# A selective-scan layer: partial sums of its products made by an accumulating DMA, in a new order

## The chip, the cores and the metric

One Trainium2 chip, of which the kernel uses one core. The time is the device time of one execution in microseconds (us), as the median of several runs. TensorE, VectorE (DVE), ScalarE (ACT), GpSimd (POOL) and SyncE (SP) each run their own list of instructions in order and wait for each other on semaphores.

## The reference, cut to what matters

2048 tokens (2 sequences of 1024) with 128 features pass through four layers, each followed by a layer norm. The first is a Mamba layer, and most of the time goes there:

```
x_and_res = x @ in_proj_w.T;  xi, res = split(x_and_res)          # 256 channels each
xi = silu(causal_depthwise_conv(xi));  dt, Bm, Cm = split(xi @ x_proj_w.T)
delta = softplus(dt @ dt_proj_w.T + dt_proj_b)
for each token t:  h = exp(delta_t * A) * h + delta_t * Bm_t * xi_t     # 256 channels x 16 states
                   y_t = sum over the 16 states of h * Cm_t
y = (y + xi * D) * silu(res);  return y @ out_proj_w.T
```

Then come a small quantised matmul, a second state layer with one shared set of 16 states, and a network of experts: a router (softmax, the two largest of 8), for each expert gelu(h Wg) * (h Wu) Wd, and a side network for tokens beyond an expert's capacity.

## The kernel before, in words

The tokens are cut into 4 chunks of 512, with the channels or features on the 128 partitions. A chunk's Mamba layer has 2 halves of 128 channels with 16 states each: 32 units, `g = 32 * chunk + k`, 128 in all. One unit is:

- GpSimd `step` (L999): drive = du * B row, a 128x512 product, into one of 6 buffers (`DRIVES`)
- ScalarE `step` (L865): decay = exp(delta * rate), into one of 3 PSUM banks `ps_state` (`RING`)
- VectorE `step` (L1127): the scan over the 512 tokens, into `ps_state`, or into `drive` where GpSimd multiplies
- VectorE `finish` (L1144), or GpSimd `multiply` (L1020) for every fourth unit of chunk 0 and every third of the others (`MULTIPLIED`): product = state * C row, into `product[:, g % 8]`. In chunks 0 and 2 the last state is also copied into `carry` (L1140, L1023)
- TensorE `finish` (L626): adds the product to the sum over the states by a matmul with the identity, in the PSUM bank `ps_y`. An addition is two matmul records in the trace. After 16 of them VectorE's `gated` (L1150) takes the sum

A product buffer is free for unit g + 8 when TensorE has added unit g (`added`). B and C rows are copied to all partitions by DMAs of SyncE (L524), two units to a transfer, 128 x 2 x 512 x 4 bytes = 512 KB, with 4 buffers each; SyncE waits for a free C buffer before it issues the next B row.

Around this run `pre` (what the scans need), `tail` (16 steps: out projection, norms, second and third layer, router), `gate`, `up` and `down` with VectorE's `join` (L1298) and `accum` (L1311) (the experts and the side network, 9 networks a chunk), and `fin` (last norm and store). Names such as tail 2.11 mean step 11 of chunk 2; gate 2.0 is the first gate of chunk 2, and it needs tail 2.13's logits, which need the normalised tokens of tail 2.11, transposed (tail 2.11 of TensorE, L683) and copied (tail 2.12 of ScalarE, L789). A decay of ScalarE needs the bank that the product three units before has read.

What order the parts take on each engine is written out in a table, `PLACES`: for each part of each chunk a list of places, and `run` sorts all parts of an engine by them. They are ranks and no times. With `PAIRED` empty, `pair` does nothing in this kernel, and `absorbed` and `paired` are false for all units.

Of the kernel before, what the change touches and what calls it, by code (L numbers as in the profile page):

```python
# [11 lines left out]
ALU = mybir.AluOpType  # L12
# [8 lines left out]
CHUNKS = TOKENS // CHUNK  # L21
# [21 lines left out]
PAIRED = (NONE, NONE, NONE, NONE)  # L43
# [18 lines left out]
for _k, _w in PARAMS.items():  # L62
# [130 lines left out]
    },  # L193
}
# [1197 lines left out]
```

## Time and profile before

| | |
|---|---|
| median of 3 runs | 480.37 us (479.71 to 483.02) |
| the profiled execution's own time | 480.05 us |
| its span, first to last instruction | 478.3 us |
| mean granted clock of TensorE, as a share of 2.4 GHz | 0.934 |
| busy: TensorE, VectorE, ScalarE, GpSimd | 407.7, 408.9, 319.4, 230.5 us |
| units of the first layer | 128, from about 35 to 378 us of the span |

The profile is of one execution. All durations in it stand against its own time of 480.05 us, of which 1.75 us lie outside the span. Busy time of an engine says how much it does, not whether anybody waits for it; that is read from the waits and from the stages.

### The profile page before, as it was taken

The page shows a single profiled execution, that of the slowest core. Times are in us where ns is not written, and L with a number is a line of the kernel's source. Part 1 is how long each engine was busy: PE and PEld are TensorE (multiplying, and loading weights), DVE is VectorE, ACT ScalarE, POOL GpSimd, SP SyncE. Part 2 cuts the span into 40 slices and gives each one's busy share as a digit, 9 for nine tenths or more (in the row PEclk, how much of TensorE's full clock was granted, in tenths as well). Part 3 has the DMA queues.
Part 4 walks back from the last instruction along what each step waited for, and adds up shares of the span by engine and source line. Part 5 has one row for each costly group of instructions (what it writes and reads, how often), then busy time and mean ns, then how long its engine had stood idle before and what let it go on. Part 6 is the DMA issues. An engine that isn't in the chain of part 4 may idle for free.

```text
span 478.3 us, 6017 instructions
## 1 busy us (share of the span) xinstructions
PE 407.7 (85%) x1680; PEld 246.4 (52%) x1680; DVE 408.9 (85%) x890; ACT 319.4 (67%) x521; POOL 230.5 (48%) x203
## 2 busy tenths in 40 slices
PE   4989777679268999999967799999496999999993
PEld 3333222243124777755423478766132687778873
DVE  4569999999999999999999889999989765675654
ACT  3887246458544999999963778874746579587231
POOL 0049599899574475456964724656962000000000
PEclk9989989999597999999997599999789899999997
DMA  8496398998245455556853723575750000000000
GB/s 288 168 332 223 110 302 292 320 311 277 86 176 187 166 175 177 181 161 194 275 185 105 248 88 120 165 229 158 251 200 2 0 1 0 3 0 23 1 1 22
DMA packets 22065, 74.19 MB, mean 155 GB/s; under 512 B 2320, under 2 KB 4368, under 8 KB 21648
## 3 DMA queue, kind: packets, MB, share of 16 engines
q1 hardware_dynamic: 22032, 73.82, 46.7%
q8 instruction: 13, 0.21, 0.2%
q14 instruction: 20, 0.16, 0.1%
HBM read 72.50 MB, written 1.31 MB: 154 GB/s over the span
## 4 chain that ended last, share of the span: by engine, by line
PE 50%; DVE 26%; issue 11%; ACT 7%; POOL 4%; DMA 2%; SPq 1%; DVEq 0%; ACTq 0%; POOLq 0%
PE ps_g L719 11%; PE ps_y L626 10%; PE ps_u L764 10%; DVE ps_state L1127 7%; PE ps_u L719 6%; DVE product L1144 4%; PE ps_state L719 2%; DMA hidden<-w_up 2%; DVE drive L1127 2%; POOL drive L999 2%; DVE delta L1111 2%; DVE delta L1113 2%; PE ps_y L764 1%; POOL product L1020 1%; DVE stats L1154 1%
## 5 line engine op out<-in xcount | busy, mean ns | idle before, releaser
L999 POOL TENSOR_TENSOR drive<-du,b_row 128x512 f32<-128x512 f32 x128 | 164.9, 1308 | 51.0 <-DVE ps_state L1127 37.3
L626 PE MATMUL ps_y<-product,par 128*128 128x512 f32 x256 | 135.6, 648 | 21.1 <-DVE product L1144 12.7
L865 ACT ACTIVATE ps_state<-delta,decay_rate 128x512 f32<-128x512 f32 x128 | 85.5, 688 | 58.3 <-DVE product L1144 45.2
L626 PEld LDWEIGHTS ps_y<-product,par 128*128 128x128 f32 x256 | 47.9, 204 | 81.8 <-issue 32.7
L782 ACT ACT_TABLE_LOAD x69 | 88.5, 1283 | 1.9 <-PEq L1385 0.7
L1020 POOL TENSOR_TENSOR product<-drive,c_row 128x512 f32<-128x512 f32 x38 | 48.4, 1274 | 55.3 <-DVE drive L1127 51.3
L1144 DVE TENSOR_TENSOR product<-ps_state,c_row 128x512 f32<-128x512 f32 x90 | 60.2, 679 | 1.3 <-PE ps_y L626 1.0
L764 PEld LDWEIGHTS ps_u<-wd,hidden 128*128 128x128 f32 x448 | 53.8, 192 | 4.9 <-issue 2.0
L1127 DVE TENSOR_TENSOR_SCAN ps_state<-ps_state,carry,drive 128x512 f32<-128x512 f32 x44 | 55.3, 1274 | 0.3 <-ACT ps_state L865 0.3
L1127 DVE TENSOR_TENSOR_SCAN ps_state<-ps_state,drive 128x512 f32<-128x512 f32 x46 | 54.6, 1213 | 0.9 <-ACT ps_state L865 0.8
L764 PE MATMUL ps_u<-wd,hidden 128*128 128x128 f32 x448 | 54.9, 276 | 0.0
L1311 DVE SCALAR_TENSOR_TENSOR acc<-ps_u,net_weight,acc 128x128 f32<-128x128 f32 x128 | 35.7, 342 | 8.3 <-PE ps_u L764 8.0
L958 ACT ACTIVATE gelu<-ps_g 128x512 f32<-128x512 f32 (+1 forms) x42 | 24.6, 595 | 21.4 <-PE ps_g L719 17.1
L719 PE MATMUL ps_g<-hn_part,wg 128*128 128x512 f32 x114 | 34.4, 419 | 0.0
L1298 DVE TENSOR_TENSOR hidden<-gelu,ps_g 128x512 f32<-128x512 f32 x36 | 24.4, 683 | 11.7 <-PE ps_g L719 4.8
L719 PE MATMUL ps_g<-hn_part,wu 128*128 128x512 f32 x108 | 33.2, 419 | 0.1
L983 POOL TENSOR_TENSOR du<-delta,u 128x512 f32<-128x512 f32 x8 | 10.6, 1330 | 33.8 <-DVE delta L1116 33.3
L1127 DVE TENSOR_TENSOR_SCAN drive<-ps_state,carry,drive 128x512 f32<-128x512 f32 x20 | 25.4, 1271 | 0.0
L719 PEld LDWEIGHTS ps_g<-hn_part,wg 128*128 128x128 f32 x114 | 21.0, 190 | 7.6 <-ACT gelu L958 1.3
L719 PEld LDWEIGHTS ps_g<-hn_part,wu 128*128 128x128 f32 x108 | 19.3, 190 | 6.3 <-issue 1.8
L1127 DVE TENSOR_TENSOR_SCAN drive<-ps_state,drive 128x512 f32<-128x512 f32 x18 | 21.8, 1210 | 0.0
L1298 DVE TENSOR_TENSOR hidden<-gelu,ps_u 128x512 f32<-128x512 f32 (+1 forms) x24 | 16.3, 679 | 6.0 <-PE ps_u L719 3.8
(253 smaller groups left out, 600.5 us busy)
## 6 DMA issues: line engine op xcount, KB each, us to landing
b_row<-bc_dram SPq DMA_DIRECT2D x64, 512.0 KB, 5.0
c_row<-bc_dram SPq DMA_DIRECT2D x64, 512.0 KB, 4.1
x_in<-x_t SPq DMA_DIRECT2D x4, 256.0 KB, 6.9
gelu<-w_gate SPq DMA_DIRECT2D x1, 1024.0 KB, 9.1
hidden<-w_up SPq DMA_DIRECT2D x1, 1024.0 KB, 10.9
wd<-w_down SPq DMA_DIRECT2D x1, 1024.0 KB, 12.8
out<-acc SPq DMA_DIRECT2D x4, 256.0 KB, 2.4
par<-params SPq DMA_DIRECT2D x1, 598.0 KB, 6.6
```

Of the source, the lines that this page charges most:

```text
L626: mm(ps_y[:, :], ident, product[:, g % PRODUCTS, :], start=False, stop=(n == STATE - 1)).then_inc(y_pe, 1)
L719: last = mm(net_bank(c, e, kind, f)[:, :], w_in[kind][wp][:, e, f * P:(f + 1) * P], hn_parts[hp][:, :], start=(i == 0), stop=(i == 2))
L764: last = mm(block_of(out_bank(c, e)[:, :], j), hidden[:, m % 2, f, j * P:(j + 1) * P], wd[:, e, f, :], start=(f == 0), stop=(f == 1))
L782: nc.scalar.preload_act_table_set(name)
L865: nc.scalar.activation(ps_state[g % RING][:, :], delta[:, c % 2, h, :], ACT.Exp, scale=decay_rate[:, h, n:n + 1]).then_inc(decay_act, 1)
L958: nc.scalar.activation(gelu[0:rows, m % GROUP, f, :], net_bank(c, e, "wg", f)[0:rows, :], ACT.Gelu).then_inc(gelu_act, inc)
L999: nc.gpsimd.tensor_tensor(drive[:, g % DRIVES, :], du[:, h, :], b_row[:, m % ROWS, n % 2, :], ALU.mult).then_inc(drive_pool, 1)
L1020: nc.gpsimd.tensor_tensor(product[:, g % PRODUCTS, :], drive[:, g % DRIVES, :], c_row[:, m % ROWS, n % 2, :], ALU.mult).then_inc(product_p ...
L1127: v.tensor_tensor_scan(drive[:, g % DRIVES, :] if multiplied(g) else state[:, :], state[:, :], drive[:, g % DRIVES, :], 0.0 if first else ...
L1144: v.tensor_tensor(product[:, g % PRODUCTS, :], state[:, :], c_row[:, m % ROWS, n % 2, :], ALU.mult).then_inc(product_dve, 1)
L1298: v.tensor_tensor(hidden[0:rows, m % 2, f, :], gelu[0:rows, m % GROUP, f, :], net_bank(c, e, "wu", f)[0:rows, :], ALU.mult).then_inc(hidde ...
L1311: last = v.scalar_tensor_tensor(acc[:, j, :], block_of(out_bank(c, e)[:, :], j), net_weight[:, j, e:e + 1], acc[:, j, :], ALU.mult, ALU.add)
```

## The change

`SUMMED` names 6 of a chunk's 8 groups of four units (0, 1, 2, 4, 5, 6; the last group of each half is left out). In such a group, once all four products are made, GpSimd issues one DMA that adds the products of units 2 and 3 of the group onto those of units 0 and 1, in SBUF. TensorE adds the two sums instead of four products. The semaphores `sum_in` (two, in turn) tell when the transfer has landed: TensorE's first two additions of a group wait for it, and so does whoever writes the buffers of units 2 and 3 again. `gated` waits for TensorE's count. The order on all five engines is new.

```diff
-PAIRED = (NONE, NONE, NONE, NONE)
+QUAD = 4
+SUMMED = ((0, 1, 2, 4, 5, 6),) * CHUNKS
...
-        pair_pool = sem("pair_pool")
+        sum_in = [sem(f"sum_in{i}") for i in range(2)]
...
+        def in_quad(g):
+            return g % UNITS // QUAD in SUMMED[g // UNITS]
+
         def absorbed(g):
 
-            return g % UNITS + 1 in PAIRED[g // UNITS]
+            return in_quad(g) and g % QUAD >= QUAD // 2
...
         def paired(g):
-            return g % UNITS in PAIRED[g // UNITS]
+            return in_quad(g) and g % QUAD < QUAD // 2
+
+        def quad(g):
+            return in_quad(g) and g % QUAD == 0
+
+        def quad_summed(eng, g):
+
+            i = count(quad, g) - 1
+            eng.wait_ge(sum_in[i % 2], 16 * (i // 2 + 1))
...
             if absorbed(g):
-                eng.wait_ge(pair_pool, count(paired, g + 1))
+                quad_summed(eng, g)
...
                 if paired(g):
-                    pe.wait_ge(pair_pool, count(paired, g))
+                    quad_summed(pe, g)
...
-                mm(ps_y[:, :], ident, product[:, g % PRODUCTS, :], start=False, stop=(n == STATE - 1)).then_inc(y_pe, 1)
+                mm(ps_y[:, :], ident, product[:, g % PRODUCTS, :], start=False,
+                   stop=(n == STATE - 1 or (in_quad(g) and n == STATE - QUAD // 2 - 1))).then_inc(y_pe, 1)
...
-                if not paired(g):
+                if not (in_quad(g) and g % QUAD == QUAD - 1):
                     return
-                made(pool, g - 1)
-                made(pool, g)
-                nc.gpsimd.tensor_tensor(product[:, g % PRODUCTS, :], product[:, (g - 1) % PRODUCTS, :],
-                                        product[:, g % PRODUCTS, :], ALU.add).then_inc(pair_pool, 1)
+                for i in range(QUAD):
+                    made(pool, g - i)
+                at, i = (g - QUAD + 1) % PRODUCTS, count(quad, g) - 1
+                if i >= 2:
+                    pool.wait_ge(sum_in[i % 2], 16 * (i // 2))
+                nc.gpsimd.dma_start(product[:, at:at + QUAD // 2, :], product[:, at + QUAD // 2:at + QUAD, :],
+                                    accum_op=ALU.add).then_inc(sum_in[i % 2], 16)
...
-                added(dve, UNITS * c + STATE * (h + 1) - 1)
+                dve.wait_ge(y_pe, count(summed, UNITS * c + STATE * (h + 1) - 1))
```

The new `PLACES`, as the orders that come out of them (s: step, f: finish, m: multiply, p: pair, a: accum, j: join; parts that do nothing are left out). VectorE in chunk 0, before and after:

```
before  s0.7 s0.8 s0.9 f0.8 f0.9 s0.10 s0.11 f0.10 s0.12 s0.13 f0.12 f0.13 s0.14 s0.15 f0.14 s0.16 s0.17 gated0.0 f0.16
after   s0.7 s0.8 s0.9 f0.8 f0.9 s0.10 s0.11 f0.10 s0.12 s0.13 s0.14 f0.12 f0.13 f0.14 s0.15 s0.16 s0.17 s0.18 f0.16
```

GpSimd in chunk 0 and at the start of chunk 1, before and after (du: `make_du`):

```
before  s0.11 s0.12 m0.7 s0.13 s0.14 s0.15 du1.0 m0.11 s0.16 s0.17 s0.18 s0.19 m0.15 s0.20 s0.21 s0.22 s0.23 s0.24 m0.19
after   s0.11 s0.12 du0.1 m0.7 p0.7 s0.13 s0.14 s0.15 m0.11 du1.0 p0.11 s0.16 s0.17 s0.18 m0.15 s0.19 s0.20 s0.21 s0.22 s0.23 m0.19 s0.24 p0.19
after   s1.4 s1.5 m1.2 s1.6 s1.7 p1.3 s1.8 m1.5 s1.9 s1.10 s1.11 p1.7 s1.12 s1.13 tail0.2 m1.8 s1.14 s1.15 s1.16 du2.0 m1.11 p1.11
```

TensorE at its first additions, and at the last ones of chunk 3:

```
before  pre1.5 f0.0 f0.1 f0.2 pre1.6 pre1.7 f0.3 pre2.0 pre2.1 f0.4
after   pre1.5 pre1.6 pre1.7 pre2.0 pre2.1 f0.0 f0.1 f0.4
before  tail2.11 f3.28 tail2.12 tail2.13 f3.29 f3.30 gate2.0 gate2.1 up2.0 up2.1 tail2.14 tail2.15 f3.31 gate2.2 gate2.3 tail3.0
after   f3.28 tail2.8 tail2.9 tail2.10 f3.29 f3.30 f3.31 tail2.11 tail2.12 tail2.13 gate2.0 gate2.1 tail2.14 tail2.15 tail3.0 tail3.1 up2.0
```

VectorE at the last products of chunk 3:

```
before  tail2.11 f3.27 s3.28 s3.29 f3.28 s3.30 tail2.12 f3.30 tail2.13 s3.31 tail2.14 f3.31 j2.0 tail2.15 gated3.1 j2.1 tail3.1
after   tail2.7 s3.28 s3.29 f3.28 tail2.8 s3.30 s3.31 tail2.9 f3.30 tail2.10 f3.31 tail2.11 gated3.1 tail2.12 tail2.13 tail2.14 tail2.15 tail3.1 j2.0
```

## Rows read from the trace of the kernel before

**Rows 1.** The page: busy us, share of the span, instructions.
```profile
PE 407.7 (85%) x1680; PEld 246.4 (52%) x1680; DVE 408.9 (85%) x890; ACT 319.4 (67%) x521; POOL 230.5 (48%) x203
```

**Rows 2.** Busy time by stage: stretch and its length, engines, then the columns named.
```profile
core 0: us, PE busy (x) PEld busy (x) DVE busy (x) ACT busy (x) POOL busy (x), PEclk, DMA share, GB/s
40.00:130.00 90.00, 64.19 (x157) 25.56 (x158) 87.97 (x132) 50.53 (x83) 76.87 (x69) 0.94 0.76 246
130.00:378.60 248.60, 222.70 (x909) 133.81 (x909) 236.31 (x494) 183.37 (x291) 142.62 (x121) 0.92 0.51 166
378.60:478.30 99.70, 91.21 (x546) 73.54 (x544) 60.28 (x206) 58.63 (x103) 1.09 (x1) 0.96 0.02 6
180.00:200.00 20.00, 20.00 (x104) 15.48 (x103) 19.34 (x38) 19.72 (x23) 9.15 (x8) 1.00 0.62 195
```

**Rows 3.** VectorE's waits, 130 to 378.6 us: us in total, times, longest.
```profile
DVE late L1267 <- PE ps_u L700: 1.7, 3, 1.1
DVE logits L1232 <- PE ps_g L688: 1.4, 1, 1.4
DVE hidden L1298 <- PE ps_g L719: 1.1, 2, 0.9
```

**Rows 4.** The additions' records (ns min/median/max), and four in the timeline (start, us).
```profile
L626 PE MATMUL ps_y<-product,par x256: 590/593/1222, 40.9 to 378.6; 128*128 128x512 f32 x128
...
88.14 1.98 PE L626 MATMUL ps_y<-product,par 128*128 128x512 f32 x4 [0.41 <-DVE product L1144]
```

**Rows 5.** The page's groups: busy us, mean ns of one, idle time before.
```profile
L999 POOL TENSOR_TENSOR drive<-du,b_row 128x512 f32<-128x512 f32 x128 | 164.9, 1308 | 51.0 <-DVE ps_state L1127 37.3
...
L1020 POOL TENSOR_TENSOR product<-drive,c_row 128x512 f32<-128x512 f32 x38 | 48.4, 1274 | 55.3 <-DVE drive L1127 51.3
L1144 DVE TENSOR_TENSOR product<-ps_state,c_row 128x512 f32<-128x512 f32 x90 | 60.2, 679 | 1.3 <-PE ps_y L626 1.0
...
L1127 DVE TENSOR_TENSOR_SCAN ps_state<-ps_state,drive 128x512 f32<-128x512 f32 x46 | 54.6, 1213 | 0.9 <-ACT ps_state L865 0.8
```

**Rows 6.** Busy time in two stretches of 12 us, columns as in rows 2.
```profile
66.00:78.00 12.00, 8.00 (x17) 2.53 (x16) 11.67 (x21) 6.26 (x9) 11.41 (x11) 1.00 0.99 313
90.00:102.00 12.00, 7.47 (x21) 2.92 (x20) 12.00 (x18) 4.91 (x8) 11.90 (x13) 1.00 1.01 335
```

**Rows 7.** From issue to landing: the B rows' transfers, then the C rows'.
```profile
DMA to landing us min/median/max: 3.9/5.0/9.8
...
DMA to landing us min/median/max: 3.3/4.1/10.5
```

**Rows 8.** The timeline of all engines, 71 to 88 us.
```profile
71.86 5.06 POOL L999 TENSOR_TENSOR drive<-du,b_row 128x512 f32<-128x512 f32 x4
72.27 0.38 SPq L524 DMA_DIRECT2D b_row<-bc_dram  x1
...
77.44 1.27 POOL L999 TENSOR_TENSOR drive<-du,b_row 128x512 f32<-128x512 f32 x1 [0.52 <-DMA b_row<-bc_dram]
...
87.35 0.15 DVE L1140 COPY carry<-ps_state 128x1 f32<-128x1 f32 x1
```

**Rows 9.** VectorE's timeline around the last product.
```profile
365.44 0.15 DVE L1221 SCALAR_TENSOR_TENSOR rms_inv<-mean_sq,rms 128x4 f32<-128x4 f32 x1
...
370.38 0.67 DVE L1229 TENSOR_TENSOR hn_part<-ps_u,hn_part 128x512 fp32r<-128x512 f32 x1
...
375.57 0.19 DVE L1262 TENSOR_TENSOR picked<-pick 128x32 bf16<-128x32 f32 x1
375.68 0.69 DVE L1144 TENSOR_TENSOR product<-ps_state,c_row 128x512 f32<-128x512 f32 x1
377.31 0.69 DVE L1298 TENSOR_TENSOR hidden<-gelu,ps_g 128x512 f32<-128x512 f32 x1 [0.95 <-PE ps_g L719]
```

**Rows 10.** Timeline of ScalarE and TensorE: x3's normalisation, and gate 2.0.
```profile
368.96 1.52 ACT L876 ACTIVATE x<-ps_g,shift,rstd 128x128 f32<-128x128 f32 x4
...
374.00 1.45 PE L719 MATMUL ps_u<-hn_part,wg 128*128 128x512 f32 x3
```

More of the change, by code:

```diff
@@ L137 @@
     "gpsimd": {
[20 rows of a table removed]
[20 rows of a table added]
     },
     "vector": {
-        "tail 0": (0, 12.2105, 12.9123, 13.0526, 14.4561, 14.7368, 14.8772, 16.7018, 17.5439, 17.9649, 18.2456, 18.6667, 19.3684, 19.5088, 19.9298, 20.3509),
+        "tail 0": (0, 13.0526, 13.7544, 13.8947, 14.8772, 15.1579, 15.2982, 16.7018, 17.5439, 17.9649, 18.2456, 18.6667, 19.6491, 19.9298, 20.2105, 20.6316),
         "split": (0.1404, 0.2807, 0.4211, 0.5614, 0.7018, 0.8421, 0.9825, 1.1228),
         "delta 0": (1.2632, 1.4035),
[2 rows of a table removed]
[2 rows of a table added]
         "delta 1": (-12.6316, -12.2105),
[26 rows of a table removed]
[26 rows of a table added]
         "fin 3": (15.7193, 15.8596),
```

182 rows, old and new, of the table PLACES are left out of this document.

## The prediction, made before the result was known

> **What bounds the kernel now.** I read the page's busy line first: TensorE and VectorE are both busy 85% of the span, 407.7 and 408.9 us [rows 1], so an average doesn't say which of them sets the end. The busy time by stage does [rows 2]. From 40 to 378.6 us, while the 128 state scans run, VectorE is idle only 2.0 and 12.3 us. From 378.6 us to the end it is idle 39.4 us, while TensorE is busy 91.2 of 99.7. So two engines take turns: VectorE bounds the scans, TensorE bounds what follows (the expert networks of chunk 2, the tail of chunk 3 and its networks). Even in the row from 180 to 200 us, where TensorE shows no idle time at all, VectorE is busy 19.34 of 20: TensorE keeps up. The waits of VectorE from 130 to 378.6 us say what it waits for: the largest that name TensorE are 1.7, 1.4 and 1.1 us [rows 3], and all seven that name it in that answer sum to 6.7 us.
>
> **What is removed.** 6 groups in each of 4 chunks lose 2 of their 4 additions on TensorE: 48 additions, 96 of the 256 matmul records of this line. A record reads 593 ns, but they overlap: four take 1.98 us [rows 4], so an addition is 1.0 us and TensorE loses 48 us of work. None of it lies behind 378.6 us: the additions end with the scans. The stage that TensorE bounds thus gets nothing directly, and the stage that loses the work is VectorE's. What can be won there is VectorE's idle time, at most 2.0 + 12.3 = 14.3 us and at least 0. I take 4 us: of the 6.7 us that name TensorE, the wait for logits and the like are a chain's latency and not its load.
>
> **What moves.** In the new order all additions of chunk 3 stand ahead of the first gate of chunk 2 on TensorE, and on VectorE the last product of chunk 3 stands ahead of the step tail 2.11 and of the router of chunk 2 (2.12 to 2.14). Before, these overlapped the scans. Let T be the end of the last product, 375.68 + 0.69 = 376.4 us [rows 9]. Before, gate 2.0 started at 374.0 [rows 10], 2.4 us ahead of T, and from there to the span's end are 104.3 us, of which 1.0 is the last addition: 103.3. After, gate 2.0 comes behind a chain that starts at T: rms scale and shift, the normalisation on ScalarE, the transpose, the copies, x3. In the trace this chain runs from 365.44 [rows 9] to the end of x3 at 368.96 + 1.52 = 370.5 [rows 10], 5.0 us, and the gate came 8.6 us after its start, having waited for other work. I take 6. The end is then T + 109.3 instead of T + 101.9: +7.4 us. Against that VectorE has less to do ahead of T: 19 rows of split, logits and routing, 370.38 to 375.57, with 3.7 us of their own, and the first join, 0.69 with a wait of 0.95 ahead of it [rows 9]: -5.3 us. The sum is +2.1 us, between +1.1 (chain of 5.0) and +4.7 (chain of 8.6).
>
> Other moves have one answer: the decays, stores, loads and pre steps keep their neighbours on SyncE and ScalarE within a few places, and the four pre steps of chunks 1 and 2 that now precede the first addition delay it by work that VectorE doesn't wait for (it has eight product buffers). I cost them at nothing; what hides them is VectorE's own queue.
>
> **What is added.** GpSimd issues 24 transfers, each adds 512 KB onto 512 KB. Three costs, none with a row of its own.
>
> (1) The issue on GpSimd. The nearest row is SyncE's issue, 0.38 us [rows 8]; the other end is one of GpSimd's own 128x512 instructions, 1.31 us [rows 5]. I take 1.0, nearer to the latter, since that row is of the same engine. Behind it on GpSimd are the drives that VectorE's scans need. In chunk 0 and the start of chunk 1 GpSimd has no room: busy 11.41 and 11.90 of 12 us [rows 6]. A group of four costs it 4 x 1.31 + 1.27 = 6.5 us and VectorE 4 x 1.21 + 3 x (0.68 + 0.15 for the carry copy) = 7.3 us [rows 5, 8]. Nine issues fall there (six of chunk 0, three of chunk 1): 9 us, less a lead of two or three drives (3 us) and less the difference of 0.8 us a group where the rows leave any idle. That puts about 4 to 5 us on VectorE; from 0 to 9.
>
> (2) The landing. Four products must be made, the transfer must land, TensorE must add the first sum (1.0 us), and only then is the group's first buffer free for the product eight places later. For the tightest group, products 4 to 7 of chunk 0: between scan 0.7 and product 0.12 VectorE now has 7 scans and 3 products, 8.5 + 2.5 = 11.0 us. From this go the multiply on GpSimd and the drive or du ahead of it, 2.6 us, and the addition: 7.4 us are left for issue and landing. Others of the dense stages have 7.4 to 9, those beside networks more. A load of the same 512 KB lands in 5.0 us (rows of B) or 4.1 (rows of C), between 3.3 and 10.5 [rows 7]. The new one reads twice, and from 66 to 102 us the DMA engines' busy share is 0.99 in the first 12 us and 1.01 in the last 12 [rows 6]. I take 7.5, a median load and half again, near the limit: 0 to 1 us of stall in each of four or five groups, 2 us together. The bounds of the landing are 3.3 and 2 x 5.0 + 2.5 = 12.5.
>
> The Trainium skill (DMA: Bandwidth & Descriptors, Anatomy of one DMA) fits a transfer issued by GpSimd by 2.0 us plus its bytes at 436 GB/s; as an estimate from that page 512 KB would land in 3.2 us and the landing would cost nothing. The trace's loads of that size, issued by SyncE, show more, and the rows decide.
>
> (3) The other loads. Each is issued only when a C row pair is free, and GpSimd already waits for one: the drive at 77.44 waited 0.52 us for a load issued at 72.27 [rows 8]. A transfer between them delays them by 1 to 3 us. Counted in (1): the lead that is used up is the same.
>
> Sum: +7 us for (1) to (3), from 0 to 30. GpSimd's wait for the partners of a group falls beside VectorE's next scans, as drives are up to six ahead.
>
> **Sum.** The profiled execution took 480.05 us, 1.75 more than its span, and stands 0.07% under the median of the three runs (480.37). 480.05 - 4 + 2.1 + 7 = 485.2, to the median scale 485.5 us, 1.1% slower. A measurement here can't tell under 1%, that is 475.6 to 485.2.
>
> **Rivals.** A, covered (0.29): landing below 7.4 us and issues near 0.38; 9 x 0.38 = 3.4 us fit into GpSimd's lead. Then 480.4 - 4 + 2.1 = 478.5, between 476 and 481. For it: GpSimd's six buffers and the sparse stages, where it is idle most of the time. Against it: two rows with GpSimd full.
>
> B, relief pays (0.13): all 14.3 us of VectorE's idle time go, nothing stalls: 480.4 - 14.3 + 2.1 = 468.2; it counts as faster from 7 us of idle time removed. For it: TensorE's row without idle time [rows 2]. Against it: VectorE is 97% busy beside it, and the last 100 us stay.
>
> C, the landing sets the pace (0.20): with 12 us the tight groups stall by 4 to 5 us each, five in chunks 0 and 1 and four later ones by about 3: 22 + 12 = 34, less (2) and most of (1): 480.4 - 4 + 2.1 + 34 = 512. It decides from 7.4 us on. For it: two reads, a full queue share, and loads that took 10.5 us [rows 7]. The Trainium skill (same page, Issuing engines are not separate DMA queues) says that transfers from all engines interleave on the same 16 engines; by that rule the loads slow the new transfers and are slowed, which would favour this case. All data of this trace go through one queue, so it can't show it.
>
> D, the clock takes it back: TensorE in the scans has less to do, and one record of this line took 1222 ns instead of 593 [rows 4], the lower of its two levels. All remaining 80 additions at that level would cost TensorE 80 x 1.0 us of the 48 it won; but in VectorE's stage. It adds 1 us to a group's landing and is part of C.
>
> **How the numbers follow.** The forecast (stalls of 3 to 12 us, 481 to 491) has 0.38, A 0.29, B 0.13, C 0.20. Faster by over 1%: B and a little of A, 0.15. Slower: 0.24 of the forecast and C, 0.44. Within: 0.41. The range leaves out half of B and the upper half of C: 473 to 506.
>
> **What the profile would show.** The addition's matmul records fall from 256 to 160; VectorE's busy time stays at 409 us; TensorE's falls to about 360, with more stretches at the lower clock. From the last product to the end: 109 us, with a gap on TensorE of 5 to 7 us right behind the last addition. New waits in chunks 0 and 1: product or drive behind the transfer or TensorE's addition, and scans behind GpSimd's drive. Landings of 6 to 9 us. Wrong I would be by a landing far from 7.5 us, or by scans that wait for nothing.

## The result and the profile after

| | before | changed |
|---|---|---|
| median | 480.12 us (479.71 to 483.02, 4 runs) | 530.01 us (527.14 to 530.88, 4 runs) |
| span of the profiled execution | 478.3 | 527.8 |
| end of the last product (T), and from there to the span's end | 376.4, 101.9 | 415.75, 112.05 |
| mean granted clock of TensorE | 0.934 | 0.853 |

The ratio is 1.106, with a 95% interval from 1.1002 to 1.1118: 10.6% slower, 50 us, where 1.1% was forecast and 506 us was the upper end of the range. 39.4 of the 49.5 us of span lie ahead of T. Ratios here and below compare undisturbed executions of both kernels alone, so they need not be the quotient of the two medians.

The page of the changed kernel, busy time [rows 1], then the groups that answer to [rows 5] and the new ones, and what its issues take to land (KB each, median us):

```profile
PE 384.5 (73%) x1584; PEld 236.1 (45%) x1584; DVE 415.5 (79%) x890; ACT 320.0 (61%) x521; POOL 248.6 (47%) x227
...
L1012 POOL TENSOR_TENSOR drive<-du,b_row 128x512 f32<-128x512 f32 x128 | 165.9, 1347 | 72.3 <-DVE ps_state L1143 50.9
L638 PE MATMUL ps_y<-product,par 128*128 128x512 f32 x160 | 101.5, 763 | 79.8 <-DMA product<-product 77.9
L878 ACT ACTIVATE ps_state<-delta,decay_rate 128x512 f32<-128x512 f32 x128 | 85.0, 686 | 78.2 <-DVE product L1160 68.8
...
L1160 DVE TENSOR_TENSOR product<-ps_state,c_row 128x512 f32<-128x512 f32 x90 | 60.3, 680 | 21.4 <-PE ps_y L638 21.3
...
L1048 POOL DMA_DIRECT2D product<-product x24 | 21.1, 881 | 7.5 <-DVE product L1160 6.8
...
b_row<-bc_dram SPq DMA_DIRECT2D x64, 512.0 KB, 6.0
c_row<-bc_dram SPq DMA_DIRECT2D x64, 512.0 KB, 5.0
product<-product POOLq DMA_DIRECT2D x24, 512.0 KB, 8.7
```

No engine is busy above 79% now; before, two were at 85%. TensorE has 96 matmul records less, as meant, but stands 77.9 us until a transfer has landed, and VectorE's products wait 21.3 us for TensorE (1.0 before). The chain that ended last names the transfers as its largest line:

```profile
DMA product<-product 18%; PE ps_y L638 9%; PE ps_g L732 6%; PE ps_u L777 5%; DVE ps_state L1143 4%; DMA b_row<-bc_dram 4%; PE ps_u L732 4%; POOL drive L1012 2%; ACT L795 2%; DVE product L1160 2%; PE ps_state L732 2%; DVE delta L1125 2%; POOL product L1033 1%; PE ps_g L603 1%; PE ps_y L777 1%
```

The windows of the dense stage and of the end, columns as in [rows 2]:

```profile
40.00:130.00 90.00, 45.52 (x94) 19.01 (x93) 72.90 (x105) 37.10 (x54) 70.42 (x67) 0.72 0.82 247
...
415.75:527.80 112.05, 99.74 (x585) 80.32 (x584) 65.34 (x235) 67.97 (x119) 1.09 (x1) 0.93 0.02 5
```

From 40 to 130 us VectorE is idle 17.1 us instead of 2.0, and the granted clock is 0.72 instead of 0.94: TensorE has become the one that waits. How one group of four does that is seen in the timeline, at the place that the prediction called the tightest (start, length in us, and in brackets the idle time before and what ended it):

```profile
60.70 0.88 POOL L1048 DMA_DIRECT2D product<-product  x1 [0.18 <-POOL carry L1036]
...
65.40 3.45 DVE L1143 TENSOR_TENSOR_SCAN ps_state<-ps_state,drive 128x512 f32<-128x512 f32 x3
...
70.56 3.78 PE L638 MATMUL ps_y<-product,par 128*128 128x512 f32 x4 [12.48 <-DMA product<-product]
...
72.16 1.26 POOL L1012 TENSOR_TENSOR drive<-du,b_row 128x512 f32<-128x512 f32 x1 [0.96 <-DMA b_row<-bc_dram]
...
72.74 0.69 DVE L1160 TENSOR_TENSOR product<-ps_state,c_row 128x512 f32<-128x512 f32 x1 [3.83 <-PE ps_y L638]
73.35 0.15 DVE L1156 COPY carry<-ps_state 128x1 f32<-128x1 f32 x1
73.47 0.69 ACT L878 ACTIVATE ps_state<-delta,decay_rate 128x512 f32<-128x512 f32 x1 [6.65 <-DVE product L1160]
```

Issued at 60.70, landed by 70.56 (9.9 us). TensorE then adds four records in 3.78 us, where [rows 4] show 1.98: it comes out of 12.5 idle us at the lower of its two levels (granted clock 0.50 in these 3.78 us, 1.00 in the 1.98 us). So the first buffer is free 12.0 us after the issue. VectorE ran out of other work at 68.9, 8.2 us after it, and loses 3.83 us; ScalarE's decays wait for that product in turn.

### The profile page after: what moved, and what is told of

Read it like the earlier page. It is cut to its first block, busy times and chain, and to the rows that moved or that the text cites. A ratio compares the mean times of both kernels' runs of the same rounds, so it can differ in the third digit from the quotient of the medians.

```text
span 527.8 us, 5897 instructions
## 1 busy us (share of the span) xinstructions
PE 384.5 (73%) x1584; PEld 236.1 (45%) x1584; DVE 415.5 (79%) x890; ACT 320.0 (61%) x521; POOL 248.6 (47%) x227
## 4 chain that ended last, share of the span: by engine, by line
PE 36%; DMA 23%; DVE 18%; issue 9%; ACT 8%; POOL 5%; POOLq 0%; DVEq 0%; SPq 0%; ACTq 0%
DMA product<-product 18%; PE ps_y L638 9%; PE ps_g L732 6%; PE ps_u L777 5%; DVE ps_state L1143 4%; DMA b_row<-bc_dram 4%; PE ps_u L732 4%; POOL drive L1012 2%; ACT L795 2%; DVE product L1160 2%; PE ps_state L732 2%; DVE delta L1125 2%; POOL product L1033 1%; PE ps_g L603 1%; PE ps_y L777 1%
## 5 line engine op out<-in xcount | busy, mean ns | idle before, releaser
L638 PE MATMUL ps_y<-product,par 128*128 128x512 f32 x160 | 101.5, 763 | 79.8 <-DMA product<-product 77.9
L638 PEld LDWEIGHTS ps_y<-product,par 128*128 128x128 f32 x160 | 34.5, 237 | 129.7 <-DMA product<-product 96.2
L1160 DVE TENSOR_TENSOR product<-ps_state,c_row 128x512 f32<-128x512 f32 x90 | 60.3, 680 | 21.4 <-PE ps_y L638 21.3
L1033 POOL TENSOR_TENSOR product<-drive,c_row 128x512 f32<-128x512 f32 x38 | 49.9, 1313 | 43.9 <-DVE drive L1143 27.8
L732 PE MATMUL ps_g<-hn_part,wg 128*128 128x512 f32 x114 | 36.8, 439 | 0.0
L732 PE MATMUL ps_g<-hn_part,wu 128*128 128x512 f32 x108 | 31.8, 407 | 0.1
L996 POOL TENSOR_TENSOR du<-delta,u 128x512 f32<-128x512 f32 x8 | 11.8, 1480 | 35.7 <-DVE delta L1132 35.4
L1143 DVE TENSOR_TENSOR_SCAN drive<-ps_state,carry,drive 128x512 f32<-128x512 f32 x20 | 25.3, 1267 | 0.0
L732 PEld LDWEIGHTS ps_g<-hn_part,wg 128*128 128x128 f32 x114 | 22.1, 201 | 7.2 <-issue 1.2
L1048 POOL DMA_DIRECT2D product<-product x24 | 21.1, 881 | 7.5 <-DVE product L1160 6.8
## 6 DMA issues: line engine op xcount, KB each, us to landing
wd<-w_down SPq DMA_DIRECT2D x1, 1024.0 KB, 12.6
```

The source lines that it names most:

```text
L638: mm(ps_y[:, :], ident, product[:, g % PRODUCTS, :], start=False, stop=(n == STATE - 1 or (in_quad(g) and n == STATE - QUAD // 2 - 1))).th ...
L732: last = mm(net_bank(c, e, kind, f)[:, :], w_in[kind][wp][:, e, f * P:(f + 1) * P], hn_parts[hp][:, :], start=(i == 0), stop=(i == 2))
L1033: nc.gpsimd.tensor_tensor(product[:, g % PRODUCTS, :], drive[:, g % DRIVES, :], c_row[:, m % ROWS, n % 2, :], ALU.mult).then_inc(product_p ...
L1143: v.tensor_tensor_scan(drive[:, g % DRIVES, :] if multiplied(g) else state[:, :], state[:, :], drive[:, g % DRIVES, :], 0.0 if first else ...
L1160: v.tensor_tensor(product[:, g % PRODUCTS, :], state[:, :], c_row[:, m % ROWS, n % 2, :], ALU.mult).then_inc(product_dve, 1)
```

## The experiments

The kernel before ran beside each of these on the same chip, with medians of 478.6 to 480.1 us. Unless said, the kernels start from the changed one. The intervals of the ratios reach 0.5 to 1.2% to each side, 3 to 6 us, and the kernels ran on several chips. Where a difference of two medians and the same difference by the ratios (of 480 us) are apart, both are given.

**The order alone** (e1_order).

```diff
-SUMMED = ((0, 1, 2, 4, 5, 6),) * CHUNKS
+SUMMED = ((),) * CHUNKS
```

> The changed kernel with no group summed: the new order alone, all 128 additions on TensorE, no transfer by GpSimd. Theory L (the landing of 8.7 us holds the product buffers and TensorE): nearly all of the 49.9 us goes, 477 to 484 us. Theory O (the new order itself costs the time): 500 us or more. Either way the time from the last product to the end should be about 109 to 112 us, against 101.9 before.

Measured 504.73 us, ratio 1.0527 (1.0455 to 1.0598), as theory O had it. Half of the loss is there without any transfer, with the end segment at 109.9 us.

**The order and the relief, no transfers** (e8_free), and **the same relief in the old order** (e9_free_old, from the kernel before).

```diff
-                quad_summed(eng, g)
+                made(eng, g)
...
-                if paired(g):
-                    quad_summed(pe, g)
-                else:
-                    made(pe, g)
+                made(pe, g)
...
-                for i in range(QUAD):
-                    made(pool, g - i)
...
-                nc.gpsimd.dma_start(product[:, at:at + QUAD // 2, :], product[:, at + QUAD // 2:at + QUAD, :],
-                                    accum_op=ALU.add).then_inc(sum_in[i % 2], 16)
+                return
```

> The changed kernel without the transfers: TensorE adds two of a summed group's four products and waits for them alone; the other two are left out of the sum, and their buffers are free once made. It is the change with a landing of zero. If the order alone costs 24.7 us (504.7 in the run with all additions): 498 us or more. If that cost came from the 48 additions that the order has no room for: 480 to 490 us. The difference to the changed kernel (530) is what the transfers cost as a whole.

> The kernel before, in its own order, with the same 48 additions left out of the sum and no transfer: what TensorE's relief is worth at best. VectorE bounds the scans: 474 to 481 us. The relief pays (rival B): 466 to 472 us. Fewer matmuls let the clock fall and that costs more than the relief gives: 481 us or more.

Measured 492.39 us in the new order, ratio 1.0337 (1.0243 to 1.043), between the two expectations, and 480.55 in the old, 1.0072 (1.0018 to 1.0125). Where nothing else is changed, 48 additions less on TensorE gain nothing: the relief is worth 0 by the medians, and by the ratio it costs 0.7%, 3 us. The granted clock is then 0.870 instead of 0.934; that the clock costs these 3 us, as one expectation had it, is not shown. In the new order the same 48 are worth 12.3 us (504.73 - 492.39; 9 by the ratios), so the new order is one that has less room on TensorE; without transfers it costs 11.8 us against the old one with the same relief (492.39 - 480.55; 12.6 by the ratios). Of the 9.6 us between the profiled spans of the two (489.7 and 480.1) the end segment has 7.9 (109.5 against 101.6). The window from the last product to the end, of the kernel before and of e8_free:

```profile
376.37:478.30 101.93, 93.44 (x566) 75.07 (x566) 61.26 (x208) 59.05 (x104) 1.09 (x1) 0.96 0.02 6
...
380.22:489.70 109.48, 97.81 (x586) 78.22 (x584) 65.32 (x235) 67.89 (x119) 1.09 (x1) 0.95 0.02 6
```

What the new order costs ahead of T is seen in VectorE's waits. From 35 us to T its scans wait 9.1 us for ScalarE's decays in e8_free and 1.5 us in e9_free_old. The longest of these waits, in e8_free:

```profile
116.83 1.50 ACT L886 ACTIVATE x<-ps_u,shift,rstd 128x128 f32<-128x128 f32 x4 [0.43 <-DVE shift L1170]
118.21 0.58 ACT L799 COPY low<-ps_u 96x512 f32<-96x512 f32 x1
118.81 1.28 ACT L792 ACT_TABLE_LOAD   x1
120.11 0.69 ACT L875 ACTIVATE ps_state<-delta,decay_rate 128x512 f32<-128x512 f32 x1
120.93 2.47 DVE L1134 TENSOR_TENSOR_SCAN ps_state<-ps_state,carry,drive 128x512 f32<-128x512 f32 x2 [4.14 <-ACT ps_state L875]
```

The same place in the kernel before:

```profile
108.30 1.28 ACT L865 ACTIVATE ps_state<-delta,decay_rate 128x512 f32<-128x512 f32 x2
110.42 2.45 DVE L1127 TENSOR_TENSOR_SCAN ps_state<-ps_state,carry,drive 128x512 f32<-128x512 f32 x2
110.54 1.50 ACT L876 ACTIVATE x<-ps_u,shift,rstd 128x128 f32<-128x128 f32 x4 [0.43 <-DVE shift L1163]
```

The new order has put two decays behind a layer norm's scaling (`x`), where the old one has them ahead of it, and VectorE stands 4.1 us. The changed kernel has the same wait (4.4 us). An order with only these decays put back was not tried.

**Transfers in the old order** (e2_oldorder02, from the kernel before). In chunks 0 and 2 only, 12 transfers; TensorE adds a group's two sums where the old order has its third and fourth addition.

```diff
+SUMMED = ((0, 1, 2, 4, 5, 6), (), (0, 1, 2, 4, 5, 6), ())
...
+                if paired(g):
+                    return
+                if absorbed(g):
+                    g, n = g - QUAD // 2, n - QUAD // 2
+                    quad_summed(pe, g)
```

> The transfers of chunks 0 and 2 (12 of 24) in the order of before: GpSimd issues each right behind the group's last multiply or six drives behind its last product, and TensorE adds the two sums in the places of units 2 and 3. If each transfer costs about 1 us by its landing (25 us for 24): 490 to 495 us. If the order of before has no room for the landing: 500 us or more. If the new order is what hurts: under 488.

Measured 550.8 us, ratio 1.1575 (1.1462 to 1.1688): 70 us for 12 transfers, against 25.3 for 24 in the new order (530.01 - 504.73). TensorE waits 81.6 us in 9 waits, with a landing of 9.2 us at the median. The new order is thus a mitigation: it costs 12 us and makes a transfer far cheaper than at the places chosen here. Other places for the issue and the sums in the old order, and all four chunks in it, were not tried.

**Room in the ring** (e3_ring12). Twelve product buffers; the low halves of the second four experts' weights are split late, into the place of the first four, for the room.

```diff
-PRODUCTS = 8
+PRODUCTS = 12
```

> The changed kernel with 12 product buffers in place of 8; to make room, the low halves of the weights are kept for four experts only (the second four overwrite them), so the experts' result is less exact, with as many matmuls as before. All 24 transfers stay. Theory L1 (what hurts is that a product waits for its buffer): VectorE's product no longer waits for TensorE (21.3 us now), 485 to 500 us. Theory L2 (what hurts is TensorE standing in its queue at the wait for the transfer, 77.9 us, with pre, tail and gate steps behind): little changes, 515 to 530 us.

Measured 526.86 us, ratio 1.0933 (1.0837 to 1.1029), 3 us less by the medians and 6 by the ratios, whose intervals overlap (the changed kernel's begins at 1.1002). With four more buffers VectorE's products wait 2.4 us for TensorE instead of 21.3, yet TensorE still waits 67.1 us for landings, and `gated`, which needs TensorE's last addition, now stands 9.8 us. Buffers alone are not what is short; TensorE's list is in order, and all behind the waiting addition, `pre` and the other additions, waits with it.

**The same with TensorE's additions one group later** (e10_defer, on top of e3_ring12).

```diff
+                if n >= QUAD and in_quad(g - QUAD) and g % QUAD < QUAD // 2 and (in_quad(g) or g % QUAD == 0):
+                    for d in range(1 if in_quad(g) else QUAD // 2):
+                        quad_summed(pe, g - QUAD + d)
+                        mm(ps_y[:, :], ident, product[:, (g - QUAD + d) % PRODUCTS, :], start=False, stop=False).then_inc(y_pe, 1)
+                if in_quad(g):
+                    return
```

> Twelve product buffers (the low halves of four experts' weights are split late to make room) and all 24 transfers, but TensorE adds a group's two sums one group later in its own queue, where the next group's first two additions stand. If the loss is TensorE standing in its in-order queue until a transfer has landed (it waited 54 to 78 us for landings in the runs with transfers), most of the 37 us between the kernel without transfers and the changed kernel go: 497 to 510 us, and TensorE's waits for DMA fall under 20 us. If the loss is the traffic of the transfers, or GpSimd's issues, the time stays at 520 to 532 us.

Measured 515.29 us, ratio 1.0777 (1.0685 to 1.087): 11.6 us less than with the ring alone (7.5 by the ratios), 14.7 less than the changed kernel (13.6). That lies between the two expectations. TensorE's waits for landings fell from 67.1 to 32.3 us, in six waits, not to under 20; the products' wait for TensorE is as small as with the ring alone. The later addition with eight buffers was not tried, so the 14.7 us belong to both together:

```profile
L635 PE MATMUL ps_y<-product,par 128*128 128x512 f32 x96 | 60.2, 756 | 32.3 <-DMA product<-product 32.3
...
L1162 DVE TENSOR_TENSOR product<-ps_state,c_row 128x512 f32<-128x512 f32 x90 | 60.1, 680 | 2.5 <-PE ps_y L635 2.4
```

**A shorter landing** (e4_quarter, e5_copy). A quarter of the columns, then a plain copy without the addition.

```diff
-                nc.gpsimd.dma_start(product[:, at:at + QUAD // 2, :], product[:, at + QUAD // 2:at + QUAD, :],
+                nc.gpsimd.dma_start(product[:, at:at + QUAD // 2, 0:128], product[:, at + QUAD // 2:at + QUAD, 0:128],
```

```diff
-                nc.gpsimd.dma_start(product[:, at:at + QUAD // 2, :], product[:, at + QUAD // 2:at + QUAD, :],
-                                    accum_op=ALU.add).then_inc(sum_in[i % 2], 16)
+                nc.gpsimd.dma_start(product[:, at:at + QUAD // 2, :], product[:, at + QUAD // 2:at + QUAD, :]).then_inc(sum_in[i % 2], 16)
```

> The changed kernel with transfers of the first 128 of 512 columns only: 128 KB each, so three quarters of the sums lack two products. Issue, semaphores and waits stay. Theory L: landing 4 to 5.5 us, 482 to 492 us. Theory G (GpSimd's issue of 0.88 us and its place in GpSimd's full queue set the loss): 515 us or more, as 24 issues stay.

> The changed kernel with plain copies in place of the accumulating transfers: same bytes written, same issue, the products of units 0 and 1 are lost. It prices the second read. If the accumulation makes the landing long: 5.5 to 6.5 us and 495 to 505 us. If the queueing beside the loads makes it: 8 us or more and 520 to 530 us.

Measured 508.67 us (1.060, 1.053 to 1.067) and 508.52 us (1.0598, 1.0518 to 1.0679), outside all four expectations. The transfers land in 6.2 and 7.5 us, medians, against 8.7. Both are 3 us above the 505.43 us of e12_traffic below, where nobody waits for a landing, and the changed kernel is 24.6 above it. The copy's issue is also shorter on GpSimd, 591 ns instead of 876 at the median, so not all of the 21.5 us that it gains can be put on the landing, and its waits cost more than these 3 us (the table at the end of this section); the quarter's issue is longer, 1202 ns, and it gains as much.

**Transfers that nobody waits for** (e12_traffic), and **the same with 16 KB** (e13_issue). TensorE adds two of four products, as in e8_free, and 24 accumulating transfers at the same places go to a buffer that no engine reads.

```diff
-                nc.gpsimd.dma_start(product[:, at:at + QUAD // 2, :], product[:, at + QUAD // 2:at + QUAD, :],
+                nc.gpsimd.dma_start(aside[:, i % 2, :, :], wd[:, 0:4, :, :].rearrange("p (a e) f d -> p a (e f d)", a=2),
                                     accum_op=ALU.add).then_inc(sum_in[i % 2], 16)
```

> The new order with two of four products left out (492.4 us without transfers), and at the places of the 24 transfers GpSimd issues 24 accumulating transfers of 512 KB into a buffer that no engine reads; GpSimd still waits for the group's four products before each, nobody waits for a landing but the second next transfer. It leaves out half of the summed products' additions, so its output is not the sum. It prices issue and traffic alone. If the wait for the landing is the cost: 493 to 500 us. If traffic slows the B and C rows, and GpSimd's issues its drives: 510 us or more. Between them the 37 us are shared in that proportion.

> As the kernel of transfers that no engine waits for, but each transfer adds 16 of 512 columns (16 KB instead of 512 KB), so GpSimd's 24 issues and its waits for a group's products stay and nearly all the traffic goes. Two of four products are left out of the sum as there. The full transfers took 505.4 us, no transfers 492.4. If the 13 us are GpSimd's issues (24 x 0.9 = 21.7 us of its time): 500 to 506 us. If they are the traffic that delays the B and C rows: 491 to 497 us, GpSimd's wait for B rows back under 10 us and the B rows' landing back at about 5 us.

Measured 505.43 us (1.0542, 1.0463 to 1.0622) and 504.2 us (1.0567, 1.045 to 1.0683). So 13 of the 37.6 us between e8_free and the changed kernel come without anybody waiting for a sum (10 by the ratios; 11.8 from e8_free to e13_issue, on one chip), 24.6 with the wait. The expectation for 16 KB had the 13 us either on the issues or on the B rows. The B rows did what the second theory asked (landing 4.9 us, GpSimd's wait for them 7.9 us, against 6.2 and 24.3 with full transfers), and the median stayed: most of it is the issues, with GpSimd's waits for a group's products ahead of them, 2.1 and 1.5 us. They aren't quite the same issues, 1202 ns at the median instead of 874, which is 8 to 10 us more of GpSimd; a share of the traffic may hide in that. The profiled executions point to one: scans wait 4.4 us for GpSimd's drives with full transfers and 0.6 us with small ones, and the spans are 503.3 and 499.1 us. Where the 13 us go was in no theory. VectorE is busy 410.4 us in e8_free, 419.9 and 419.2 in these two, with the same 890 instructions. One operation in e12_traffic's timeline, beside GpSimd:

```profile
45.42 0.95 POOL L1049 DMA_DIRECT2D aside<-wd  x1
...
46.16 5.16 POOL L1011 TENSOR_TENSOR drive<-du,b_row 128x512 f32<-128x512 f32 x4
46.90 5.94 DVE L1128 TENSOR_SCALAR delta<-sp_exp 128x512 f32<-128x512 f32 x1
51.16 1.38 POOL L995 TENSOR_TENSOR du<-delta,u 128x512 f32<-128x512 f32 x1
52.87 0.69 DVE L1130 TENSOR_TENSOR delta<-sp_exp,delta 128x512 f32<-128x512 f32 x1
```

The same operation in the kernel before, at the same place and once more:

```profile
44.20 8.49 POOL L999 TENSOR_TENSOR drive<-du,b_row 128x512 f32<-128x512 f32 x6
...
46.87 1.34 DVE L1109 TENSOR_SCALAR delta<-sp_exp 128x512 f32<-128x512 f32 x1
53.83 0.41 DVE L1109 TENSOR_SCALAR delta<-sp_exp 128x512 f32<-128x512 f32 x1
```

It takes 0.41 us undisturbed and 1.34 beside the six drives of the kernel before, which stand without a gap too: there it gets its turn behind one of them. In e12_traffic it takes 5.94 us, until all five GpSimd instructions behind the issue are done. So a full GpSimd alone doesn't do it. What differs is that GpSimd's records behind an issue overlap, one starting some 0.3 us before the one ahead has ended (35 of the 41 pairs of e12_traffic that follow an issue without idle time, by over 0.1 us; none of 106 pairs in the kernel before). Why is not shown. The changed kernel has the same at this place (3.55 us) and at 289.64:

```profile
289.52 0.85 POOL L1048 DMA_DIRECT2D product<-product  x1
289.64 4.76 DVE L1125 TENSOR_SCALAR delta<-sp_exp 128x512 f32<-128x512 f32 x1
290.13 3.98 POOL L1012 TENSOR_TENSOR drive<-du,b_row 128x512 f32<-128x512 f32 x3
294.31 1.26 POOL L1012 TENSOR_TENSOR drive<-du,b_row 128x512 f32<-128x512 f32 x1 [0.20 <-POOL drive L1012]
```

The Trainium skill (SBUF — State Buffer, SBUF: two separate sides) says that VectorE in some of its forms and GpSimd share a pair of ports that one of them holds for a whole instruction while the other is blocked. The trace agrees with the blocking: the 1.34 us of the kernel before fit one instruction, and in 5.94 us VectorE stood aside for several GpSimd instructions in a row.

**Only the late transfers** (e6_late). 15 of 24.

```diff
-SUMMED = ((0, 1, 2, 4, 5, 6),) * CHUNKS
+SUMMED = ((), (4, 5, 6), (0, 1, 2, 4, 5, 6), (0, 1, 2, 4, 5, 6))
```

> The new order and transfers, but none in chunk 0 and none in the first four groups of chunk 1: 15 transfers stay, those of the stages where networks stand between the units; the others add four products each on TensorE. The new order without any transfer took 504.7 us, all 24 took 530. If the loss is in the dense stages, where VectorE has seven scans and three products to a buffer: 503 to 510 us. If every transfer costs about the same (25.3/24 = 1.05 us each): 520.5 us.

Measured 509.38 us, ratio 1.0635 (1.0559 to 1.0711). Against the order alone, 15 transfers beside networks cost 4.7 us, 0.3 each; the nine in the dense stages the other 20.6, 2.3 each. Both are net of the additions that the transfers save.

**A warm TensorE** (e7_warm). Two matmuls with zero weights ahead of each wait for a transfer.

```diff
+                    if quad(g):
+                        if g == 0:
+                            pe.wait_ge(pool_const, 4)
+                        for _ in range(QUAD // 2):
+                            mm(ps_y[:, :], zeros[:, :], x_in[:, 0, TAPS - 1:TAPS - 1 + CHUNK], start=False, stop=False)
```

> The changed kernel with two more matmuls ahead of TensorE's wait for each transfer, with a matrix of zeros as weights, so that they add nothing: TensorE has as many matmuls as before. If the lower granted clock (0.72 from 40 to 130 us) is a large part of the loss: 505 to 520 us and a clock above 0.9. If the landing alone is: 528 to 535.

Measured 532.21 us, ratio 1.117 (1.1049 to 1.1291). The mean clock rose from 0.853 to 0.891, in the dense stage from 0.72 to 0.77, and the time did not fall. The clock follows from the waiting and isn't the main cause; a stage at full clock throughout wasn't reached, so what the rest of the lower clock costs stays open.

**VectorE up to T, in all of them.** The profiled executions, VectorE's busy and idle time from the start to T, in us:

| kernel | landing | T | busy | idle |
|---|---|---|---|---|
| before | none | 376.4 | 347.6 | 28.8 |
| e9_free_old | none | 378.5 | 348.3 | 30.3 |
| e8_free | none | 380.2 | 345.1 | 35.1 |
| e13_issue | 5.4, no one waits | 389.9 | 353.9 | 36.0 |
| e12_traffic | 8.6, no one waits | 393.5 | 354.6 | 38.9 |
| e4_quarter | 6.2 | 396.6 | 355.8 | 40.9 |
| e5_copy | 7.5 | 395.3 | 348.2 | 47.1 |
| e10_defer | 8.9 | 400.4 | 348.1 | 52.3 |
| changed | 8.7 | 415.8 | 350.2 | 65.6 |

Over e8_free, VectorE is busy 3 to 11 us longer where GpSimd issues transfers. Its idle time grows by 1 to 4 us where nobody waits for a landing, and by up to 30 where TensorE does. The copy is idle 8 us longer than e12_traffic and busy 6 us less, so a landing of 7.5 us costs some 8 us and not 3.

No version with transfers came near the kernel before. The fastest kernel in the new order, 492.4 us, leaves out part of the sum and is still slower.

## Why the prediction was wrong

The direction was right, and the landing works as rival C had it; the sizes were not right, and what the order costs ahead of T was left out. By the runs, the 49.9 us are: relief 0, order 12.3, issues 13.0, landing 24.6 (by the ratios 3, 13, 10 and 25). The forecast had -4, +2.1, +5 and +2. The parts come from taking things away in one sequence; in the changed kernel itself VectorE is busy 5.1 us longer than in e8_free, not 9.5 as in e12_traffic, so the line between the last two is not exact. By its steps:

- **What bounds the kernel.** Right. VectorE bounds the scans: the relief alone gave 480.55 us, no gain, where 4 us were taken and 0 was the lower bound. Rival B falls by that. In the new order TensorE does bound part of the scans: there the same relief is worth 12.3 us.
- **What moves, behind T.** Right: gate 2.0 starts at 420.90, 5.15 us after T = 415.75, where the chain was put at 6; the end segment without transfers is 109.5 us, forecast 109.3. The changed kernel's own 112.05 us go with a granted clock of 0.94 from 470 to 500 us, where e10_defer has 1.00 in the same work and 109.9 us.
- **What moves, ahead of T.** Wrong. 5.3 us of VectorE's work went behind T, but T came 3.8 us later (380.2 in e8_free) instead of 5.3 earlier, and 16.1 later when TensorE keeps all additions (392.5 in e1_order). "I cost them at nothing; what hides them is VectorE's own queue" is the step that failed: the rest of the new order was dismissed from a few places on two engines, the decays among them ("keep their neighbours on SyncE and ScalarE within a few places"). In the 90 us from 40 to 130 e8_free's VectorE is busy 81.69 us where before shows 87.97 [rows 2]. Against the old order with the same relief T comes 1.7 us later instead of 5.3 earlier, 7.0 us in all, and scans wait 7.6 us more for decays (9.1 against 1.5), 4.1 of them at one place. That these waits are the cause is read from the trace; no run took the moves apart.
- **The issue (1) and the other loads (3).** The issue was taken at 1.0 us, measured 0.88. Its price was taken at 4 to 5 us, measured 13.0. The bounds counted GpSimd's time alone. The missing term is VectorE: its instructions grow by 9.5 us in sum, with the long ones behind GpSimd's issues (410.4 to 419.9). The loads were delayed as said, B rows landing in 6.0 us instead of 5.0, and with 16 KB instead of 512 KB the median fell by no more than 1.2 us, the profiled span by 4.2. The rule that transfers of all engines interleave (the Trainium skill, DMA: Bandwidth & Descriptors, Issuing engines are not separate DMA queues) fits: B rows land in 6.2 us beside full transfers of GpSimd and in 4.9 beside small ones.
- **The landing (2).** The budget of 7.4 us was well placed, the price on both sides of it too low. VectorE's idle time up to T is 2 us more than in e12_traffic at a landing of 6.2, 8 at 7.5 and 27 at 8.7, where the forecast had 2 us in all at 7.5. The landing was taken at 7.5 and is 8.7 (5.0 to 10.4), still within the bounds of 3.3 and 12.5. The term that was mis-sized is the stall per group: rival C had 34 us at a landing of 12, and 24.6 came at 8.7. It counted from the issue to the landing and 1.0 us of addition. In the group shown the landing is 9.9 and the first sum 2.2 us behind it (70.56 to 72.74), since TensorE comes back at its lower level. And it counted VectorE's buffers only: with four more of them 3 us came back (6 by the ratios), with the additions a group later besides 14.7 (13.6). So TensorE standing in its list is a part of its own that the sum lacked. The remaining 9.9 us between e10_defer and e12_traffic weren't taken apart; TensorE still waits 32.3 us for landings there.
- **Rival D** put the clock at 1 us a group inside C. The rows agree (3.78 instead of 1.98 us for four records, mean 763 ns), and e7_warm shows no more behind it.
- **What the profile would show.** 160 records, new waits of products behind TensorE, landings of 6 to 9 us (8.7): right. The gap behind the last addition is smaller, 2.3 us of idle time between 416.9 and the gate at 420.90, not 5 to 7, since two short steps stand in it. TensorE's busy time fell by 23.2 us to 384.5, not by 48 to 360, as its remaining records are longer (763 ns against a mean of 648 before); VectorE's is 415.5, not 409.

The forecast and rival C were 27 us apart at landings of 7.5 and 12 us, with a limit at 7.4 between "nothing" and a stall in each group. A landing taken 0.1 above such a limit is not a likeliest value with a range of 3 to 12 us around it; C deserved more than 0.20, and its price had to join those of the order and the issue, since all three can come together.

## What to carry to other kernels

A wait placed in an in-order engine holds all that stands behind it: ask where the waiting instruction can stand later, since here that gave 11.6 us on top of the 3 us of four more buffers (7.5 and 6 by the ratios). A list changed "within a few places" is not the same list: follow, on each engine, what stands ahead of the work that the bounding engine needs next, as the decays here. When a sum has a limit, as 7.4 us of landing here, price both sides of it per group and don't take a value beside the limit. DMA issues given to a full GpSimd are also paid on VectorE: compare VectorE's busy time for the same number of instructions.

## What the runs showed of the hardware

- An accumulating transfer of 512 KB within SBUF, issued by GpSimd beside the row loads, lands in 8.7 us at the median; a plain copy of it in 7.5, an accumulating one of 128 KB in 6.2, of 16 KB in 5.4. A size 32 times smaller takes 3.3 us off the 8.7. The Trainium skill's fit (DMA: Bandwidth & Descriptors, Anatomy of one DMA), 3.2 us for 512 KB as an estimate, is under the shortest accumulating one of that size seen, 4.5 in e3_ring12 (5.0 in the changed kernel); the shortest plain copy took 2.9.
- GpSimd's issue takes 876 ns at the median for 512 KB accumulating, 591 for the plain copy, and more for less: 1202 for 128 KB (a quarter of each row) and for 16 KB.
- An SBUF operation of VectorE that takes 0.41 us took 5.94 beside GpSimd's instructions behind an issue and 1.34 beside as dense a row of them without one. Another of 128x4, with a median of 158 ns, took up to 5377 ns (e12_traffic):

```profile
L1182 DVE SCALAR_TENSOR_TENSOR shift<-moments,rstd x12: 136/158/5377, 122.6 to 498.4; 128x4 f32<-128x4 f32 x12
```
